# The first inverse transform by even and odd lines, and the heads' mix on quarters of the array

## The reference

```
qf = xf.reshape(b, HEADS, hd, h * w)                 # xf = fft2(x), 8 heads of 16 channels
attn_f = softmax over each head, of real and imaginary part apart
out_cplx = jnp.einsum('bhcd,bhdn->bhcn', attn_f, qf)
out_f = jnp.abs(jnp.fft.ifft2(out_cplx))
g = sigmoid(conv(relu(bn(conv(xf.real, w1, b1))), w2, b2))
out_f_l = jnp.abs(jnp.fft.ifft2(g * xf))
fsa = conv(concat([out_f, out_f_l]), projf_w)
```

## Time and profile before

| | us |
|---|---|
| median of three runs | 24949.8 |
| the profiled execution | 24943.67 |
| its span | 24941.9 |
| inverse transform, image 0 (433.8 to 529) | 95.2 |
| heads' stage, image 0 (529 to 703.6) | 174.6 |
| the same two stages, image 1 | 97.5 and 174.0 |

### The profile page before, as it was taken

How to read it: one execution, slowest core, us unless ns; L and a number is a source line. 1 busy time by engine, 2 the same in 40 slices (tenths; PEclk the granted TensorE clock), 3 DMA queues, 4 the chain that set the end, 5 groups by cost and what they waited for, 6 DMA issues and landing times.

```text
span 24941.9 us, 329327 instructions
## 1 busy us (share of the span) xinstructions
PE 22557.0 (90%) x107489; PEld 13255.3 (53%) x107489; DVE 19918.5 (80%) x23961; ACT 13275.5 (53%) x18807; POOL 12339.5 (49%) x4613
## 2 busy tenths in 40 slices
PE   5999999999999999998888888888888888888888
PEld 4777778687777777684333333333333333333333
DVE  4666657465666657468999999999999999999999
ACT  2323141323223131325777777777777777777776
POOL 0000000000000000005999999999999999999998
PEclk8999999999999999999999999999999999999999
DMA  3122221303022221304444444444444444444444
GB/s 98 42 88 74 80 82 42 120 22 107 35 91 70 81 81 46 102 25 153 168 167 189 167 192 168 168 191 168 166 190 166 187 173 168 191 167 166 191 166 165
DMA packets 866693, 3187.54 MB, mean 128 GB/s; under 512 B 68265, under 2 KB 340026, under 8 KB 579770
## 3 DMA queue, kind: packets, MB, share of 16 engines
q1 hardware_dynamic: 866234, 3181.65, 34.6%
HBM read 2884.91 MB, written 296.49 MB: 128 GB/s over the span
## 4 chain that ended last, share of the span: by engine, by line
PE 33%; DVE 9%; issue 6%; ACT 4%; DMA 2%; DVEq 0%; ACTq 0%; POOL 0%; SPq 0%; POOLq 0%
PE yp L2051 16%; PE pj L2007 8%; DVE hid L2274 4%; DVE hid L2280 3%; PE pj L2036 2%; PE pj L2066 2%; PE pj L2024 2%; PE pj L2015 2%; PE yp L2043 1%; ACT t L2133 1%; DMA img<-x 1%; DVE delta L2316 1%; DMA bc<-bc_rows 1%; ACT xn L2147 1%; ACT du L2181 1%
## 5 line engine op out<-in xcount | busy, mean ns | idle before, releaser
L2382 POOL TENSOR_TENSOR hid<-hid,bc 128x2048 f32<-128x2048 f32 x2048 | 7814.9, 3816 | 908.2 <-DVE carry L2288 905.6
L2051 PE MATMUL yp<-hid,ident 128*128 128x512 f32 x16384 | 7346.5, 597 | 428.2 <-POOL hid L2382 428.2
L2356 POOL TENSOR_SCALAR_AFFINE_SELECT ident<-ident 128x128 f32<-128x128 f32 x1 | 0.3, 295 | 11436.1 <-DVE ident L2241 11436.1
L2051 PEld LDWEIGHTS yp<-hid,ident 128*128 128x128 f32 x16384 | 3040.8, 189 | 4626.9 <-issue 3960.4
L2274 DVE TENSOR_TENSOR_SCAN hid<-da,carry,t 128x512 f32<-128x512 f32 x3968 | 4857.3, 1266 | 111.0 <-DVE carry L2288 9.7
L2280 DVE TENSOR_TENSOR_SCAN hid<-t,carry,hid 128x512 f32<-128x512 f32 x3968 | 4827.8, 1258 | 29.9 <-ACT t L2122 29.4
L2375 POOL TENSOR_TENSOR hid<-bc,du 128x1024 f32<-128x1024 f32 x2048 | 4102.0, 2003 | 196.7 <-PE yp L2051 170.5
L2122 ACT ACTIVATE t<-delta,v_a 128x512 f32<-128x512 f32 x4096 | 2660.1, 681 | 1574.0 <-DVE hid L2280 1571.0
L1202 PE MATMUL bk<-region 128*128 128x256 f16 (+2 forms) x30640 | 3379.4, 266 | 61.3 <-ACT region L1559 43.7
L2007 PE MATMUL pj<-xn,w_x 128*128 128x512 f32 x4096 | 2373.3, 733 | 1077.8 <-ACT xn L2147 1030.0
L1202 PE MATMUL bk<-work,region 128*128 128x256 f16 x27336 | 3164.8, 274 | 23.6 <-DVE region L1047 20.5
(11 more groups left out here) (288 smaller groups left out, 22499.4 us busy)
## 6 DMA issues: line engine op xcount, KB each, us to landing
bc<-bc_rows SPq DMA_DIRECT2D x1024, 2048.0 KB, 7.2
work<-in_shift_d SPq DMA_DIRECT2D x256, 512.0 KB, 3.8
work<-in_x SPq DMA_DIRECT2D x256, 256.0 KB, 2.7
work<-in_x SPq DMA_DIRECT2D x128, 512.0 KB, 5.1
xpad<-in_x SPq DMA_DIRECT2D x32, 2048.0 KB, 12.4
gated<-work SPq DMA_DIRECT2D x256, 256.0 KB, 2.4
region<-gated SPq DMA_DIRECT2D x256, 256.0 KB, 2.9
region<-heads SPq DMA_DIRECT2D x256, 256.0 KB, 3.1
```

The source lines that it names most:

```text
L2051: m = nc.tensor.matmul(yp[:, h, :], ident[:, :], hid[:, k % 4, n, :], start=False, stop=(g == G - 1 and n == 3), skip_group_check=True)
L2382: nc.gpsimd.tensor_tensor(hid[:, k % 4, :, :], hid[:, k % 4, :, :], bc[:, g, 1, :, :], ALU.mult).then_inc(s_hc.sem, 1)
```

## The change

**Inverse transform.** The tables have the lines in the order even, odd. `inverse1` no longer multiplies a full 128-row weight by 256 columns; since for an even line the two halves of the sum over the rows have the same sign, and for an odd line the opposite one, it works out two partial sums apart: each weight is split into its upper and its lower 64 rows, which are multiplied by tables of 128 columns (`ics`, `isc`) into two banks. ScalarE copies one bank (256 columns) to `Ze`, and VectorE, in the new `join`, writes their sum and difference to `Z`, two instructions of 128 x 256. `inverse2` has banks 4 and 5 alone, so it waits until both absolute values of the step before it are taken. The heads' softmax on VectorE is cut into five parts, which stand between the joins of steps 0, 3, 6, 8 and 11.

**Heads' mix.** A turn of the loop has two chunks, m and m + 16 (`place`), whose shifts are made one after the other and whose mixes are made together: each 128 x 128 weight is cut to its two 64 x 64 blocks on the diagonal (a head has 16 channels, so the other two are zero), and the four products of a block and a chunk go to the four quarters of the array. For o = 0 (real) and o = 1 (imaginary) these are 24 passes of 512 columns each. `shifted` and `sq2` have four buffers in place of two. The roots of two chunks stand together, in the first half of a turn, behind take_rows and the high half.

**Output stage.** `OF` has another layout, and `of` is loaded by four transfers of 64 partitions in place of one of 128, in pieces of 64 f32 words.

The core of the diff:

```diff
+    order = np.concatenate([i[0::2], i[1::2]])
-        "cs": np.concatenate([cos, -sin], 1), "sc": np.concatenate([sin, cos], 1),
+        "cs": np.concatenate([cos[:, order], -sin[:, order]], 1), "sc": np.concatenate([sin[:, order], cos[:, order]], 1),
+        "ics": np.concatenate([cos[order, :64], -sin[order, :64]], 1), "isc": np.concatenate([sin[order, :64], cos[order, :64]], 1),
...
-        OF = region[:, 0:HW].rearrange("p (a h) -> p a h", h=P)
+        OF = region[:, 0:HW].rearrange("p (r a h) -> p r a h", r=2, h=64)
...
+                def join(p):
+                    dve.wait_ge(s_ze.sem, s_ze.at(b, p + 1))
+                    dve.wait_ge(s_i1.sem, s_i1.at(b, p + 1))
+                    dve.wait_ge(s_i2.sem, s_i2.at(b, 2 * (p // 2) - 2))
...
+                    V.tensor_tensor(to[:, :, 0], odd, even, ALU.add)
+                    V.scalar_tensor_tensor(to[:, :, 1], odd, -1.0, even, ALU.mult, ALU.add).then_inc(s_z.sem, 1)
...
+                steps_of_heads = {0: heads_norm, 3: heads_rows, 6: heads_largest, 8: heads_soft, 11: heads_mix}
+                join(0)
+                join(1)
+                for s in range(NK // 2):
+                    if s in steps_of_heads:
+                        steps_of_heads[s]()
+                    if 2 * s + 2 < NK:
+                        join(2 * s + 2)
+                        join(2 * s + 3)
...
-                    dve.wait_ge(s_os.sem, s_os.at(b, 2 * kk + 2))
-                    V.tensor_tensor(sq2[0], sq2[0], sq2[1], ALU.add).then_inc(s_oa.sem, 1)
+                    for r in range(2):
+                        dve.wait_ge(s_os.sem, s_os.at(b, 4 * m + 3 + r))
+                        V.tensor_tensor(sq2[r], sq2[r], sq2[2 + r], ALU.add).then_inc(s_oa.sem, 1)
...
+                        if not (isinstance(n_, int) and n_ == NK - 1):
+                            turned_rows(n_ + 1)
+                        if blk == 0 and not (isinstance(m, int) and m < 2):
+                            add_squares(m - 2)
...
-                    sp.dma_start(of[par], of_d[0:1, :, bass.ds(kk * 512, 512)].rearrange("a c n -> (a c) n")).then_inc(sof[par], 16)
+                    for r in range(2):
+                        for blk in range(2):
+                            part = of[par].rearrange("p (a h w) -> p a h w", a=4, h=2)[64 * r:64 * r + 64, :, blk, :]
+                            sp.dma_start(part, of_d[0:1, 64 * blk:64 * blk + 64, bass.ds(kk * 256 + r * 8192, 256)].rearrange("a c (j w) -> (a c) j w", w=64)).then_inc(sof[par], 16)
...
-                        o = bk[p % 2][:, q * 256:(q + 1) * 256]
-                        mm(o, pairs[0][:, 2 * p + q, :], k["cs"], start=True, stop=False)
-                        m = mm(o, pairs[1][:, 2 * p + q, :], k["sc"], start=False, stop=True)
+                        for X, table, first in ((0, k["ics"], True), (1, k["isc"], False)):
+                            for half in range(2):
+                                r = slice(64 * half, 64 * half + 64)
+                                m = mm(bk[2 * (p % 2) + half][:, q * P:(q + 1) * P], pairs[X][r, 2 * p + q, :], table[r, :], start=first, stop=not first)
...
-                    pe.wait_ge(s_abs.sem, s_abs.at(b, 2 * s - 2))
+                    pe.wait_ge(s_abs.sem, s_abs.at(b, 2 * s))
...
-                    for o, terms in ((o_re, ((0, 0), (2, 1))), (o_im, ((0, 1), (1, 0)))):
-                        for n_, (w_, part) in enumerate(terms):
-                            for wh, ph in ((0, 0), (0, 1), (1, 0)):
-                                m = mm(o, mix16[:, w_, wh, :], shifted[par][:, part, ph, :], start=(n_ == 0 and wh == 0 and ph == 0), stop=(n_ == 1 and wh == 1))
+                    for n_, (w_, part) in enumerate((((0, 0), (2, 1)), ((0, 1), (1, 0)))[o]):
+                        for wh, ph in ((0, 0), (0, 1), (1, 0)):
+                            for r in range(2):
+                                rows_ = slice(64 * r, 64 * r + 64)
+                                for blk in range(2):
+                                    x_ = mm(bk[3 + 2 * o + r][64 * blk:64 * blk + 64, :], mix16[rows_, w_, wh, rows_], shifted[2 * mp + blk][rows_, part, ph, :], start=(n_ == 0 and wh == 0 and ph == 0), stop=(n_ == 1 and wh == 1))
...
-                    if not (isinstance(kk, int) and kk < 3):
-                        root(kk - 3)
...
+                        if not (isinstance(n_, int) and n_ == NK - 1):
+                            take_rows(n_ + 1, place(m, 1) if blk == 0 else place(m + 1, 0))
...
+                        cp(shifted[2 * mp + blk][:, 0, 0], bk[1][:, :], scale=HSCALE).then_inc(s_shr.sem, 1)
+                        if blk == 0 and not (isinstance(m, int) and m < 2):
+                            root(m - 2)
+                        if not (isinstance(m, int) and m == 0):
+                            squares(m - 1, blk)
```

More of the change, by code:

```diff
@@ L653, in rows_loop, with heads_loop @@
             body(NK - 1, 1)
+        NM = NK // 2
+        place = lambda m, blk: m + NM * blk
+        def heads_loop(eng, body):
+            body(0, 0)
+            body(1, 1)
+            with eng.Fori(1, NM // 2 - 1) as i:
+                body(i * 2, 0)
+                body(i * 2 + 1, 1)
+            body(NM - 2, 0)
+            body(NM - 1, 1)
         def pair_loop(eng, body):
@@ L795, in image, with largest @@
                 dve.wait_ge(s_gst, b * 16 + 16)
-                def softmax(name, width, mask):
+                def largest(name, width, mask):
                     L = sq[1][:, 0:width]
@@ L1343, in inverse2 @@
                             r = slice(64 * hf, 64 * hf + 64)
-                            m = mm(bk[2 + 2 * (s % 2) + hf][:, :], k["back"][r, part], Z[r, s % 2, :, part], start=first, stop=not first)
+                            m = mm(bk[4 + hf][:, :], k["back"][r, part], Z[r, s % 2, :, part], start=first, stop=not first)
                             if not first:
@@ L1382, in body, with mix @@
-                def body(kk, par):
-                    first, last = (isinstance(kk, int) and kk == i for i in (0, NK - 1))
-                    pe.wait_ge(s_trc.sem, s_trc.at(b, kk + 1))
-                    pe.wait_ge(s_kl[par], b * (8 * NK) + (kk - par) * 8 + 16)
-                    pe.wait_ge(s_shr.sem, s_shr.at(b, kk))
-                    pe.wait_ge(s_shi.sem, s_shi.at(b, kk))
-                    for j in range(4):
-                        for s in range(2):
-                            m = mm(bk[1 + s][:, j * P:(j + 1) * P], turned[:, j * P:(j + 1) * P], kbuf3[par][:, j, s * P:(s + 1) * P], start=True, stop=True)
-                    m.then_inc(s_sh.sem, 1)
-                    if not last:
-                        turn(kk + 1)
-                    if not first:
-                        mix(kk - 1, 1 - par)
+                def mix(m, mp, o):
+                    if o == 0:
+                        pe.wait_ge(s_shr.sem, s_shr.at(b, 2 * m + 2))
+                        pe.wait_ge(s_shi.sem, s_shi.at(b, 2 * m + 2))
+                    pe.wait_ge(s_os.sem, s_os.at(b, 4 * m - 2 + 2 * o))
+                    pe.sem_inc(s_mix.sem, 1)
+                    for n_, (w_, part) in enumerate((((0, 0), (2, 1)), ((0, 1), (1, 0)))[o]):
+                        for wh, ph in ((0, 0), (0, 1), (1, 0)):
+                            for r in range(2):
+                                rows_ = slice(64 * r, 64 * r + 64)
+                                for blk in range(2):
+                                    x_ = mm(bk[3 + 2 * o + r][64 * blk:64 * blk + 64, :], mix16[rows_, w_, wh, rows_], shifted[2 * mp + blk][rows_, part, ph, :], start=(n_ == 0 and wh == 0 and ph == 0), stop=(n_ == 1 and wh == 1))
+                    x_.then_inc(s_o.sem, 1)
@@ new lines, in body @@
+                def body(m, mp):
+                    for blk in range(2):
+                        n_ = 2 * m + blk
+                        pe.wait_ge(s_trc.sem, s_trc.at(b, n_ + 1))
+                        pe.wait_ge(s_kl[blk], b * (8 * NK) + m * 16 + 16)
+                        pe.wait_ge(s_shr.sem, s_shr.at(b, n_))
+                        pe.wait_ge(s_shi.sem, s_shi.at(b, n_))
+                        for j in range(4):
+                            for s in range(2):
+                                x_ = mm(bk[1 + s][:, j * P:(j + 1) * P], turned[:, j * P:(j + 1) * P], kbuf3[blk][:, j, s * P:(s + 1) * P], start=True, stop=True)
+                        x_.then_inc(s_sh.sem, 1)
+                        if not (isinstance(n_, int) and n_ == NK - 1):
+                            turn(n_ + 1)
+                        if not (isinstance(m, int) and m == 0):
+                            mix(m - 1, 1 - mp, blk)
@@ L1665, in image, with squares @@
-                take_rows(0)
-                rows_loop(act, body, 2)
-                root(NK - 3)
-                for kk in range(NK - 2, NK):
-                    squares(kk, kk % 2)
-                    root(kk)
+                def squares(m, o):
```

(13 more changed lines are left out.)

185 lines of the change are left out of this document (99 added, 86 removed).

## The result

The changed kernel takes 25146.68 us (median of four runs, 25135.58 to 25149.26) against 24948.45 us before: a ratio of 1.0079, 95% interval 1.0061 to 1.0096. The forecast was 25080 us, slower. The sum stands on single stages, so I read these first. The table gives the mean over the eight images, worked out from the starts of four kinds of rows in each trace: the last VectorE instruction ahead of the inverse transform (line 837, now 863), the first `turn`, the last imaginary high half (879, now 942), and the first load and last store of the output stage.

A forecast was written before the change was run, and what follows sets the result against it. PE was taken to bound the inverse transform and the heads' stage. Per image -29 (inverse), +44 (heads) and +1.5 (output) make +16.5 us, +132 over eight: 25080 us, range 24880 to 25240.

The forecast's parts named there:

- Inverse transform, -29 forecast: Inverse transform: PE's step falls from 5.57 to 3.45 us, -34 us an image, less 4 to 6 given back.
- The term for the softmax and the table loads: Inverse transform: softmax between joins, two table loads and waits of inverse2 give back 4 to 6 us an image.
- Heads' loop, +44 forecast: Heads' stage: a loop over VectorE, ScalarE and PE replaces PE as bound; +21.6, +9 and +13 us an image.
- The chain over the root: Heads' stage: loop through ScalarE's roots takes 11.66 us a pair in place of 10.12, +21.6 us an image.
- The table load before the first root: Heads' stage: 1.28 us wholly on the path in six passes, 7.7 us; with the load before take_rows, +9 an image.
- The clock: Heads' stage: PE's idle time of some 2.5 us a pair lowers its clock, 0.9 us x 14 = +13 an image.
- The upper bound of the heads' stage: Heads' stage: at most +56 us an image, before the rivals.
- The column halves: Rival, heads' mix: column halves of the array do not run side by side, 25190 to 25330 us; chance 0.10.
- the weight loads: Rival, inverse transform: half arrays' weight loads run in a row, -5 in place of -29, 25270 us; chance 0.04.
- Few falls of the clock: Rival, heads' stage: no or few clock falls, heads +31 or less, +28 us in all; chance 0.20.
- the root is not on the path: Rival, heads' stage: ScalarE's detour fits beside VectorE and PE, pairs 9.56 us, 24660 us in all; chance 0.09.
- the output stage, +1.5: Output stage: four load issues put the last 1.6 us later, about even with PE's need; +1.5 us an image.

The follow-up runs named there:

- the filler: Changed kernel plus ten unused f16 passes on PE between a pair's second shift and the next turn, table loads kept: 25052.2 us, ratio 1.0039.
- the later root: Changed kernel with ScalarE's root moved behind the second real high half, squares reordered: 24779.12 us; with a Sqrt ahead of the loop, so no table loads in it: 24745.04 us.
- the inverse part alone: Kernel before plus only the inverse transform's part of the change, heads' stage and output stage as before: 24740.51 us, ratio 0.9914.
- the fastest kernel: Changed kernel with root behind second high half, no table loads in the heads' loop, and turned copy moved from VectorE to ScalarE: 24587.59 us, ratio 0.9858.

## Why the prediction was right

- *Inverse transform, -29 forecast, -27.8 measured.* A step of 3.45 us was forecast, 3.50 came. The term for the softmax and the table loads, 4 to 6 us, was right in size: 16 x 2.07 = 33.1 would have gone, 27.8 did.
- *Heads' loop, +44 forecast, +44.0 measured.* The chain over the root: 11.66 us forecast, 11.95 came; the 0.3 is the hop from the turned copy to the second shift (586.82 to 587.21), for which I took 0.06. With 10.10 before, that is 1.85 us a pair and 24 to 26 us an image, 21.6 forecast. The table load before the first root lies on the path, as forecast, and the other one is hidden but for 0.1 us: 6 x 1.4 = 8.4 us, 9 forecast. The clock: 13 forecast, 12.1 taken away by the filler. So the three terms are off by 0.6 to 4 us each and these errors cancel in part. Of the clock the size was right and the form only in part: I had a fall of 0.9 us in each of 14 pairs, but in six of eight images, past their first passes, only the pairs with a load lose by it, 2.0 us each, and the others nothing; in the other two images nearly every pair loses about 1 us. That the first kind comes to the same 12 us as the second is luck; falls of 0.9 us came without the loads, in two pairs of three. The upper bound of the heads' stage adds up to 55, not 56. Put in another order, the loop lost all of the +44.
- *The rivals.* The column halves do run side by side (1.49 us for 24 passes), the weight loads too. Few falls of the clock: refused by 0.87. That the root is not on the path: refused by the wait of 2.65 us ahead of it with VectorE waiting 2.15 behind, but it is what the later root made true, with pairs of 9.73 us without table loads, near the 9.56 of that rival. Its 24660 us did not come: the 24745 us there are no less than the inverse part alone, since the other stages take back what the loop gains.
- *The term that was mis-sized* is the output stage, +1.5 an image forecast, +4.2 measured. The issues of a chunk, then PE and its weight loads in that chunk and PE in the next:

```profile
1439.79 0.33 SPq L1237 DMA_DIRECT2D region<-gated  x1
1440.31 2.99 SPq L1241 DMA_DIRECT2D region<-heads  x4
```

```profile
1444.08 2.11 PE L1269 MATMUL bk<-region,work 128*128 128x512 f32 x4
1445.06 0.30 PEld L1269 LDWEIGHTS bk<-region,work 128*128 128x128 f32 x2 [0.79 <-DMA region<-heads]
1456.14 1.88 PE L1269 MATMUL bk<-region,work 128*128 128x512 f32 x4
```

  The four issues start 0.79 us apart, not the 0.53 that I took, so the last is 2.4 us behind the first in place of 1.6. But each part lands about 2.3 us after its issue, in place of the 3.1 of a whole load, and the last one lands 4.7 us behind the first issue: 1.6 + 3.1, as forecast, and about even with PE's third pass. What I mis-sized is what even costs. Every second chunk is late, by 0.15 to 0.37 us (two chunks' starts on PE are 12.0 to 12.2 us apart in place of 11.83); in the chunks between, 0.2 to 0.4 us are left. Fifteen late chunks in image 0 make 3.6 us, and one that stood before as well grew by 0.3. PE's weight loads there wait 20.0 us in all for these transfers, 30 times, which is 1.7 us, once, before; most of that is hidden behind the products.
- *What was not in the sum*: 2.3 us an image between the heads' loop and the output stage, of which 2.1 lie between the last high half and the first store of `heads`, where the last two chunks' mixes, squares and roots are now made one after the other (the last 48 quarter passes, at 719.70, take 4.45 us where 24 take 1.49 at full speed, so in part at a lower clock); 0.6 in the rest, and the 19 us outside the images. With 2.7 us an image more in the output stage and 1.2 in the inverse transform these are 6.8 x 8 + 19 = 73 us, where 25080 and 25147 are 67 apart. The 19 us outside the images I can't attribute: the traces of the experiments differ among each other by 4 us ahead of the images and 8 behind them, and no run tells whether any of it belongs to the change.

The Trainium skill ("TensorEngine Tiling (Array Packing)", Key Properties) has the change of mode drain the engine. The trace agrees as to the next change: in the fastest kernel a mix and the shift behind it take 3.31 us from start to start (590.61 to 593.92), and six slots of 0.216 with 16 of 0.112 are 3.09, so 0.22 us goes to one change of shape, the 0.2 of the earlier trace rows. In the changed kernel PE is waiting anyway. The 1.38 us of drain that the Trainium skill has beside a table load ("ScalarE: Activation LUTs", What ACT_TABLE_LOAD costs) do not show in the loop: with the clock held a pass with two loads is 25.30 us against 23.90 without, 1.4 more for both, where by the Trainium skill one switch alone would be 2.66. The load that is not on the path starts at 587.70, 0.02 us behind the end of the squares (586.59 + 1.09).

## What to carry to other kernels

When the engine that bounds a stage is relieved, write down one turn of each engine's list and follow the loop through them: what is behind an instruction that waits late (here a root for a sum) becomes the bound, whatever the shares say. Moving it behind the instruction that others wait for cost nothing and was worth 368 us. Moving a copy from the engine that then closed the loop (VectorE) to the less busy one (ScalarE) was worth another 157 (24745 to 24588 us). Look in the compiled order for table loads that a new loop has taken in, and count the issues of a split transfer at their own price; a transfer that comes out even with its use in the sum is late in part of the turns.

## What the runs showed that I had not expected

- The same idle time of 2.4 us on PE was followed by half clock in some pairs and by full clock in others, in a loop whose turns are all alike; without table loads it went by threes. An idle time of 1.5 us with more work ahead of it was not followed by half clock in any pair of the steady loop, in eight images (13.34 and 11.96 us throughout).
- More work on PE made the kernel 94 us faster (ten idle f16 passes a pair, 0.87 to 0.97 of clock).
- Stores of 8 MB in pieces of 256 bytes in place of whole rows lengthened the stage behind them by 18 us an image.
